# Diffusion transformer blocks on one core: the wait for the constant rows of K stands before the first stack, and GpSimd's norm subtracts the mean without negating it

## What is computed

```
m, v = mean(x), var(x)                       # over the 128 features
h = (x - m) / sqrt(v + eps) * (1 + scale) + shift
attention: q, k, v = h @ W + b; softmax(q k^T / sqrt(8)) v, per head
           (self, windowed, over a context, or with only the 16 largest scores of each row)
x = x + gate * (attention @ Wo + bo)         # or gate * MLP(h)
```

## Time and profile before

| what | value |
|---|---|
| median of 3 runs | 673.63 us (669.01, 673.63, 683.54) |
| the profiled execution | 665.29 us |
| its span, first to last instruction | 663.5 us |
| mean granted clock of TensorE | 0.863 of full |
| busy: PE | 570.0 us, 86% |
| busy: DVE | 490.9 us, 74% |
| busy: ACT | 386.3 us, 58% |
| busy: POOL | 306.4 us, 46% |

### The profile page before, as it was taken

One profiled execution on the slowest core, in us unless ns is written; L12 is line 12 of the kernel. 1 busy time (PEld: TensorE's weight loads), 2 busy tenths in 40 slices (PEclk: granted clock), 3 DMA queues, 4 the chain that ended last, 5 costly groups with the idle time before them and its releaser, 6 DMA issues.

```text
span 663.5 us, 14489 instructions
## 1 busy us (share of the span) xinstructions
PE 570.0 (86%) x5152; PEld 378.9 (57%) x5152; DVE 490.9 (74%) x1291; ACT 386.3 (58%) x669; POOL 306.4 (46%) x584
## 2 busy tenths in 40 slices
PE   3888989899999999999998889786999987867477
PEld 3645556566756565657665556554655664634246
DVE  2577767853859687745377727999999999999953
ACT  2546878799696887886757766452233531611133
POOL 6884535435845444364562446641341446111133
PEclk9858999999999999998989979777575795765779
DMA  9560344302333533020335043140020002000000
GB/s 319 143 159 3 88 106 112 73 2 54 76 67 69 105 77 78 2 65 2 66 72 123 2 129 68 28 101 0 2 65 2 2 10 64 9 1 2 1 2 16
DMA packets 15062, 39.23 MB, mean 59 GB/s; under 512 B 2641, under 2 KB 6801, under 8 KB 14737
## 3 DMA queue, kind: packets, MB, share of 16 engines
q0 software_dynamic: 8960, 29.37, 20.1%
q1 hardware_dynamic: 5312, 8.46, 3.8%
q10 hardware_dynamic: 720, 0.49, 0.3%
HBM read 7.96 MB, written 0.52 MB: 13 GB/s over the span
## 4 chain that ended last, share of the span: by engine, by line
DVE 38%; PE 37%; ACT 8%; DMA 6%; issue 6%; POOL 4%; ACTq 0%; POOLq 0%
PE psum L1590 10%; DVE left L1419 8%; DVE left L1429 7%; DVE top L1426 6%; DVE top L1416 6%; DVE maxima L1406 5%; PE psum L1566 5%; PE psum L1536 5%; ACT softmax_T L1298 4%; DMA qk_stack<-centred 3%; PE psum L1625 3%; PE psum L1636 3%; DMA qk_stack<-qk_parts 2%; DVE maxima L1402 2%; PE psum L1617 2%
## 5 line engine op out<-in xcount | busy, mean ns | idle before, releaser
L1298 ACT ACTIVATE softmax_T<-psum 128x1024 f32<-128x1024 f32 (+1 forms) x224 | 210.9, 962 | 111.7 <-PE psum L1577 73.3
L1406 DVE TENSOR_REDUCE maxima<-psum 128x4 f32<-128x1024 f32 x160 | 190.1, 1216 | 52.4 <-PE psum L1536 51.6
L1566 PE MATMUL psum<-qk_stack 32*128 32x256 f32 (+1 forms) x896 | 114.9, 346 | 28.1 <-DMA qk_stack<-centred 9.6
L1590 PE MATMUL psum<-softmax_T,values 128*32 128x256 f32 (+1 forms) x1792 | 129.9, 408 | 4.8 <-ACT softmax_T L1298 3.5
L1566 PEld LDWEIGHTS psum<-qk_stack 32*128 32x128 f32 x896 | 72.3, 202 | 71.0 <-issue 31.0
L1227 POOL TENSOR_SCALAR unpicked<-left 128x512 bf16<-128x512 f32 x64 | 39.5, 616 | 136.0 <-DVE left L1429 135.3
L1536 PE MATMUL psum<-qk_stack 32*128 32x256 f32 (+1 forms) x768 | 89.6, 335 | 9.2 <-ACT softmax_T L1298 2.4
L1536 PEld LDWEIGHTS psum<-qk_stack 32*128 32x128 f32 x768 | 58.9, 200 | 37.5 <-issue 16.5
L1590 PEld LDWEIGHTS psum<-softmax_T,values 128*32 128x32 f32 x1792 | 56.7, 118 | 40.3 <-issue 12.0
L1187 POOL TENSOR_TENSOR qk_parts<-qk_parts 128x256 fp32r<-128x256 f32 x56 | 40.9, 730 | 77.0 <-ACT qk_parts L1281 76.6
L1158 POOL DMA_DIRECT2D qk_stack<-qk_parts x112 | 63.7, 580 | 7.0 <-POOL qk_parts L1187 6.3
(11 more groups left out here) (99 smaller groups left out, 870.3 us busy)
## 6 DMA issues: line engine op xcount, KB each, us to landing
qk_stack<-qk_parts POOLq DMA_DIRECT2D x112, 256.0 KB, 5.1
weights<-in_w SPq DMA_DIRECT2D x1, 1408.0 KB, 13.5
row_biases<-in_rows SPq DMA_DIRECT2D x1, 1088.0 KB, 10.8
weights<-in_w SPq DMA_DIRECT2D x2, 512.0 KB, 5.9
weights<-in_w SPq DMA_DIRECT2D x1, 832.0 KB, 9.0
qk_stack<-centred SPq DMA_DIRECT2D x48, 8.0 KB
weights<-in_w SPq DMA_DIRECT2D x1, 768.0 KB, 4.3
weights<-in_w SPq DMA_DIRECT2D x1, 576.0 KB, 3.7
```

Of the source, the lines that this page charges most:

```text
L1298: nc.scalar.activation(pT[:, slot, u % 2, :, 0:cols].rearrange("p (i t) n -> p i t n", t=NT), two_banks(step).rearrange("p i (t n) -> p i ...
L1406: nc.vector.tensor_reduce(rows[:, u // 4, u // 2 % 2, g:g + 2, :], ps.rearrange("p i (t k) -> p i t k", t=NT), AX_X, ALU.max).then_inc(fin, 1)
L1566: ins = nc.tensor.matmul(ps[:, i, t, 0:P if window else N], QKS[b][32 * g:32 * g + 32, s, 1, P * t:P * t + P], QKS[b][32 * g:32 * g + 32, ...
L1590: ins = nc.tensor.matmul(misc[32 * g:32 * g + 32, queries], V[:, b, t, first:first + 32], pT[:, slot, g // 2, 2 * (g % 2) + t, 0:P if wind ...
```

## The change

The wait for the constant rows moves from ahead of GpSimd's whole list to just ahead of the first `stack`. The norm no longer writes `neg_mean`: it subtracts the mean straight from `mean_var`, and the tile `neg_mean` (64 bytes in each partition) goes. The orders stay.

```diff
-        nmean = sb("neg_mean", [P, B, 2, NT])
...
             pool.wait_ge(q_zero_s, 1)
-            pool.wait_ge(k_rows_s, 16 * SLOTS["qk"])
+            first_stack = next(i for i, s in enumerate(ORDERS["pool"]) if s[0] == "stack")
             for step in ORDERS["pool"]:
                 kind, b, l, u = step
                 if kind == "stack":
                     slot = SLOT["qk", ("k_parts", b, l, 0)][0]
+                    if step == ORDERS["pool"][first_stack]:
+                        pool.wait_ge(k_rows_s, 16 * SLOTS["qk"])
...
-                    nc.gpsimd.tensor_scalar(nmean[:, b, c, :], mv[:, b, c, :, 0], -1.0, 0.0, ALU.mult, ALU.add)
                     link(nc.gpsimd.tensor_scalar(veps[:, b, c, :], mv[:, b, c, :, 1], 1.0, eps, ALU.mult, ALU.add))
                     link(nc.gpsimd.tensor_tensor(rstd[:, b, c, :], veps[:, b, c, :], half_pow[:], ALU.pow))
                     for t in range(NT):
-                        ins = nc.gpsimd.tensor_scalar(dst[:, b, t, :], src[:, b, t, :], nmean[:, b, c, t:t + 1],
-                                                      rstd[:, b, c, t:t + 1], ALU.add, ALU.mult)
+                        ins = nc.gpsimd.tensor_scalar(dst[:, b, t, :], src[:, b, t, :], mv[:, b, c, t, 0:1],
+                                                      rstd[:, b, c, t:t + 1], ALU.subtract, ALU.mult)
```

## The result

The changed kernel is slower: 677.82 us median of 20 runs (671.13 to 688.27) against 671.12 of 20 (660.40 to 683.54), ratio 1.0131 with a 95% interval of 1.0089 to 1.0173. A ratio here compares only those executions of each kernel that lie within 1.5% of its fastest; the medians of all give 1.010. The forecast was 668, with a gain of 3.4 us, and the top of its range was 678.

What follows compares the result with a forecast made beforehand. TensorE was taken to bound 64 to 300 us, VectorE 405 to 635, and a chain through the constant rows' DMA and GpSimd's norms the start. Gains of 2.4 + 1.0 = 3.4 us from 671.3 gave 668 us, range 660 to 678.

Steps and rivals of the forecast that it cites:

- the operation and the operand: GpSimd's centring: subtract for add, mean read from mean_var; 3 ns x 96, 0.3 us on an engine with room, taken as nothing.
- The operand: GpSimd's centring: the scalar is read from mean_var at every second word instead of its own tile; taken as nothing.
- The negation: GpSimd's norm: leaving out the instruction that negates the mean was said to save 0.25 us per norm.
- The wait: Start of the kernel: first norm at about 7.0 us instead of 9.48, of which 2.4 us come through to the first stack.
- The other 44 norms: Norms behind the start: each 0.25 us shorter, four of them on the chain that ended last, so 1.0 us gained.
- GpSimd is never the bound after the start: Whole kernel after the start: TensorE paces 64 to 300 us, VectorE 405 to 635 us, GpSimd no stretch.
- The rival that a worse clock makes it slower: TensorE, where it is the bound: another 26 us half-clock stretch would cost 9.5 us, giving 677.4 us; chance 0.12.
- VectorE and the shared ports: Start: earlier norms beside VectorE's modulations could delay these to 11.6 us, before ScalarE's 11.9; costed at nothing, up to 0.7 us.

Runs made afterwards that it cites:

- wait_only: Against the kernel before: only the wait for the constant rows is moved, the norm keeps its negation and addition; 667.62 us against 669.30, ratio 0.994.
- norm_only: Against the kernel before: only the norm is changed (subtracts the mean from mean_var, no negation), the wait stays first; 675.80 us against 669.30, ratio 1.0076.

## Why the prediction was wrong

- **What fell: "the operation and the operand".** The step priced subtract against add by the tensor_tensor rows (730 and 727 ns) and took "nothing, from either side". Those rows are of another instruction. On GpSimd's tensor_scalar the pair subtract, mult takes 793 ns on 128 columns where add, mult takes 447. The term should have been +0.70 us for each norm, 33.6 us of GpSimd's time, instead of 0.3 us for all of them. The error was to call a bound what was a row of a neighbour: no row of the trace held a tensor_scalar with a subtraction, so both ends should have stood open, and a centring twice as long belonged among the rivals.
- **The operand** was priced right: `mean_var`'s pairs cost nothing (L1029 and L1025 both take 2.59 us for six).
- **The negation: over-priced.** It was taken as 0.25 us a norm, the distance between two starts. Back to back, leaving it out gives 0.15 us (2.18 less 2.03).
- **The wait: right.** The first norm started at 6.91 (7.0 expected). With the norm as it was, `wait_only` shows the projection at 12.71 (12.5), ScalarE's parts at 14.66 (14.45), the stack at 18.11 (17.55). The gain is 1.9 us at the stack and 1.5 us at the norm of the earlier trace rows, and from 1.7 us (medians) to 4 us (ratio 0.994) at the end, for 2.4. In the changed kernel it went back before the first stack: the four longer norms end at 17.99 us instead of `wait_only`'s 15.99, and GpSimd is last again.
- **The other 44 norms: wrong sign.** They were to give 1.0 us back through 4 norms on the chain. They became longer, and the chain took in more of them: 10 behind the start. The sentence that GpSimd is never the bound after the start held for short norms only; its share of the chain went from 4% to 7%. Against `wait_only`, which has the same moved wait with short norms, an estimate is 14 x 0.55 = 7.7 us; measured are 1.9% of 670 by the two ratios (12.8 us) and 1.25% by the medians of all executions (8.4 us). The estimate lies near the second, and how far the rest is real the intervals don't say.
- **The rival that a worse clock makes it slower** gave 677.4 us, which is nearly the measured 677.8. That is luck. Its cause was the earlier start, and `wait_only` has the same earlier start and isn't slower, with a clock in the stretch of 0.80. `norm_only` has no earlier start and no worse a clock over its executions (0.854 against 0.849), and is slower. In the pair of traces a worse clock does go with 8.8 of the 12.1 us. Over many executions it can account for less: after's 20 have a mean clock of 0.843, which by the line above would be some 2.5 us of the 6.7, if before's clock in that set was the 0.849 of the next. That share stays open.
- **VectorE and the shared ports: right to leave out.** The modulations were done by 9.4 us (L1366 began at 9.20 in the trace after), long before ScalarE's 11.78. On GpSimd's side the first centring pair lost 0.17 us.

## What to carry to other kernels

On GpSimd, the pair of operations in a tensor_scalar decides its speed: of the pairs tried, those of add with mult and of mult with mult are quick, so negate a small operand once rather than subtract over all columns. Price an instruction only by a row of the same instruction with the same operations; where there is none, leave both ends open, or measure that one form by itself before trusting an edit that removes a cheap one. In a kernel with fixed lists, a longer step costs most where the chain passes through it; count those places before the engine's busy time. And where executions of one kernel differ by 3%, a pair of traces shows what an instruction costs, but not what the kernel gains or loses.

## What the runs showed of the hardware that was not expected

GpSimd's tensor_scalar on 128 partitions of fp32 takes 447, 554 and 767 ns at 128, 256 and 512 columns for add, mult, but 793, 1219 and 2072 ns for subtract, mult. The slow time at 128 columns (794 ns) also holds for add, add; mult, subtract; subtract, add; and subtract, subtract. With constants in place of scalars from SBUF both are 150 ns shorter at 128 columns (297 and 644 ns), and the difference of 347 ns stays.
